# A selective scan with a routed expert layer on one core: another order of VectorE's instructions, and five loads and products placed elsewhere

## The chip, the cores and the metric

One core of one Trainium2 chip runs the whole program. The metric is the device time of one execution in microseconds. In the profile PE is TensorE, DVE is VectorE, ACT is ScalarE, POOL is GpSimd and SP is SyncE, which only issues DMAs.

## What is computed

The input is 2 batch rows of 1024 tokens with 512 values, all in float32. Each token is normalised (layernorm) and goes through two branches; the output is `x + s * g`.

```python
proj = xn @ W_in.T                       # x and gate, 1024 channels each
x = silu(conv4(x))                       # four taps along time, per channel
ts, B, C = rms(x @ W_x.T)                # 32, 16 and 16 values of a token
dt = softplus(ts @ W_dt.T + b_dt)        # per channel and token
state = state * exp(dt * A) + (dt * x) * B      # 16 states of each channel
y = (state . C + x * D) * silu(gate)
s = y @ W_out.T
g = silu(sum of the token's top 2 of 8 experts, weighted by softmax)
```

## The kernel before, in words

**Tiles and quads.** The 2048 tokens are cut into 4 chunks of 512 (two chunks to a batch row), the 1024 channels into 8 groups of 128 that stand on the partitions. A tile n is one chunk c = n // 8 with one group t = n % 8, so the main loop of every engine runs over 32 tiles. A tile has 16 states to each channel. They are done in 4 quads of 4 states; m = 4n + q numbers the quads through the program. For the scan the channels of a group are spread so that 32 channels with 4 states fill the 128 partitions, and a quad is 4 instructions of 128x512 (r = 0 to 3; half 0 is r = 0, 1, the low half; half 1 is r = 2, 3, the high half).

**The life of a quad.** GpSimd makes the drives `(dt*x)*B` for the quad in one instruction (`drives`, L588) into a ring of 4 quads. ScalarE makes the decays `exp(dt*A)` into four banks `sc` of PSUM, two at a time (`decays(m, h)`, L801). VectorE scans each r along time (L1175). Then the scanned states are multiplied by C: the high half by VectorE (`products(m, 1)`, L1185), the low half by GpSimd (`low_products`, L601) where `POOL_QUADS` says so, else by VectorE. TensorE adds them over the states (`sums`, L1426). The four banks `sc` are single: the decays of half h of quad m+1 wait until that half of quad m has been read, which for the high half is the end of its product. In the first chunk of a batch row ScalarE also copies the last column of each scan into `state` (`keep_states`, L780) before it overwrites the half, and GpSimd's low product waits for that copy.

**Step sizes.** For tile n+2 TensorE projects, ScalarE does the exponential and logarithm (`softplus`), and VectorE finishes softplus with three instructions that each need the one before (`step_sizes`, L1154, L1156, L1158) and multiplies by x (`times_x`, L1150). Tiles that are not in `VECTOR_LOG` have the sum done by TensorE, and VectorE only multiplies. ScalarE stores dt and dt*x to DRAM (`keep_rows`, L849), SyncE reads them back spread over the partitions (`spread`, L406), and GpSimd's drives of the tile wait for that.

**The convolution of the next chunk.** In the tiles with t = 2 to 5 (late) and 3 to 6 (early) of the chunks 0 to 2 one group of x of the next chunk is projected by TensorE (`next_x`, L1322, from `w_x`), copied by ScalarE with the first tap (`copy_x`, L707 to L712), and VectorE adds three taps, each on the result of the one before (`convolve`, L1114). ScalarE applies Silu later, with the gate's Silu (`silu_gate`, L861), between two loads of its function table (L941, L949).

**Dependent instructions on VectorE.** Where an instruction of VectorE needs the result of an earlier one, the program waits on a semaphore that the earlier one raises (`link`, or `scan_ok` for a product). In the order before, such an instruction nearly always comes directly behind the one that it waits for: scan, scan, product; tap, tap, tap; the three parts of a step size and the multiplication.

**Each engine's order is written out by hand** in its own loop over the tiles; SyncE's queue is one such list. Of SyncE the change touches the load of `w_out` (2 MB, L474, issued in tile 2, first used in tile 8) and that of `w_x` in tile 18. There the order is: wait for `o_add` (the last sum of an output tile, made by GpSimd), a slot and an expert's weights, more slots, and then `load_w_x`. A slot is 128 gathered tokens of one expert: `x_slot` is loaded by SyncE, turned by TensorE (L1400), copied by ScalarE (L811), multiplied (L1411), copied (L820) and stored (L827). In the tiles 0 and 1 GpSimd scatters token rows into the slots (L552) between the drives.

**A tile's order on VectorE before**, which the change rewrites:

```python
low(m); [times_x(n+1)]; scans(m, 1); [step_sizes(n+1)]; products(m, 1); gate_tile(n-1)
low(m+1); [convolve(early)]; scans(m+1, 1); products(m+1, 1)
low(m+2); high(m+2); [convolve(late)]
low(m+3); high(m+3); [rms or step_sizes(n+2)]
```

## Time and profile before

| | us |
|---|---|
| median of 3 runs (1069.73 to 1072.17) | 1071.06 |
| the profiled execution, its own time | 1074.76 |
| its span, first to last instruction | 1072.9 |
| mean granted clock of TensorE | 0.906 of full speed |

The profiled execution is 3.7 us above the median of the runs and its time is 1.9 us more than its span. The profile gives for each engine the time in which it was busy, so that VectorE and GpSimd, both with high shares, must be read stretch by stretch: idle time of an engine counts only where the chain that ended last passes through what it waited for. The main loop's tiles take 24 to 36 us each.

### The profile page before, as it was taken

To read this page: it belongs to the slowest core of one execution; us is meant where nothing else is said; L and a number is where in the kernel's file an instruction comes from. 1 tells how busy PE (TensorE), PEld (TensorE's weight loads), DVE (VectorE), ACT (ScalarE), POOL (GpSimd) and SP (SyncE) were. 2 spreads that over 40 slices of the span, in tenths; PEclk is the share of its full clock that TensorE was granted. 3 is DMA by queue.
4 is the path that set the end of the run, shared out by engine and by line. 5 is a ranking of instruction groups with operands and counts; after the bars stand their busy time and mean duration, and the time that the engine had idled before them with its cause. 6 is when DMAs were issued, how large, how long until landed. Compare 5 with 4: busy or idle time off the path is not lost.

```text
span 1072.9 us, 10234 instructions
## 1 busy us (share of the span) xinstructions
PE 861.6 (80%) x2756; PEld 319.1 (30%) x2756; DVE 996.6 (93%) x1025; ACT 727.6 (68%) x1281; POOL 909.7 (85%) x322
## 2 busy tenths in 40 slices
PE   8943557988978998898846859889897999679568
PEld 5321112333323333333211313333332343223122
DVE  6779988999999989999999899999999989999997
ACT  3657656788787766788565566688777666567543
POOL 0617898997989998888798979799988988999996
PEclk9976668999999999999876879999998999889779
DMA  9847668767778576666743752965648556664725
GB/s 336 345 158 285 223 235 330 278 247 267 263 266 333 183 270 241 228 257 212 259 113 143 217 194 109 320 231 191 228 149 303 217 215 235 216 220 182 274 42 154
DMA packets 86585, 245.93 MB, mean 229 GB/s; under 512 B 9344, under 2 KB 10752, under 8 KB 79872
## 3 DMA queue, kind: packets, MB, share of 16 engines
q1 hardware_dynamic: 67712, 197.03, 51.4%
q10 hardware_dynamic: 12672, 31.46, 7.4%
q0 software_dynamic: 6144, 16.78, 5.8%
q8 instruction: 23, 0.38, 0.1%
q14 instruction: 34, 0.28, 0.1%
HBM read 183.11 MB, written 62.13 MB: 229 GB/s over the span
## 4 chain that ended last, share of the span: by engine, by line
DVE 30%; PE 22%; POOL 21%; issue 11%; DMA 9%; ACT 5%; SPq 2%; DVEq 0%; ACTq 0%; POOLq 0%
DVE sc_ps L1175 13%; POOL drive L588 12%; DVE drive L1175 8%; PE x_ps L1458 5%; POOL drive L601 4%; PE f_ps L1411 4%; DMA rep<-rep_rows 4%; PE y_ps L1426 3%; PE dt_ps L1386 2%; DMA rep_rows<-dtu 2%; DVE x_ps L1114 2%; DVE drive L1185 2%; PE x_ps L1322 2%; POOL moe L573 2%; ACT sc_ps L801 1%
## 5 line engine op out<-in xcount | busy, mean ns | idle before, releaser
L588 POOL TENSOR_TENSOR drive<-rep,b_all 128x2048 f32<-128x2048 f32 x127 | 578.9, 4598 | 46.6 <-DMA rep<-rep_rows 40.5
L801 ACT ACTIVATE sc_ps<-rep,a_neg 128x512 f32<-128x512 f32 x512 | 332.0, 681 | 93.3 <-DVE drive L1185 63.4
L601 POOL TENSOR_TENSOR drive<-drive,c_all 128x1024 f32<-128x1024 f32 x94 | 224.2, 2385 | 20.6 <-ACT state L780 12.8
L1426 PE MATMUL y_ps<-drive,stack 128*32 128x512 f32 x1024 | 153.5, 675 | 107.1 <-POOL drive L601 59.8
L1175 DVE TENSOR_TENSOR_SCAN sc_ps<-sc_ps,state,drive 128x512 f32<-128x512 f32 x164 | 201.0, 1272 | 4.7 <-ACT sc_ps L801 2.4
L1185 DVE TENSOR_TENSOR drive<-sc_ps,c_all 128x1024 f32<-128x1024 f32 x162 | 198.4, 1224 | 5.4
L1175 DVE TENSOR_TENSOR_SCAN sc_ps<-sc_ps,drive 128x512 f32<-128x512 f32 x160 | 186.5, 1211 | 14.6 <-ACT sc_ps L801 7.4
L1411 PE MATMUL f_ps<-w_ring,xT_slot 128*128 128x512 f32 x368 | 171.8, 611 | 14.9 <-ACT xT_slot L811 14.7
L1386 PE MATMUL dt_ps<-xnT,w_g 128*128 128x512 f32 x232 | 126.8, 697 | 27.5 <-ACT dtu L768 27.5
L1175 DVE TENSOR_TENSOR_SCAN drive<-sc_ps,state,drive 128x512 f32<-128x512 f32 x92 | 112.7, 1266 | 3.4 <-ACT sc_ps L801 3.4
L1175 DVE TENSOR_TENSOR_SCAN drive<-sc_ps,drive 128x512 f32<-128x512 f32 x96 | 111.7, 1205 | 0.0
L1411 PEld LDWEIGHTS f_ps<-w_ring,xT_slot 128*128 128x128 f32 x368 | 68.9, 195 | 117.4 <-issue 116.7
L1322 PE MATMUL x_ps<-xnT,w_x 128*128 128x512 f32 x192 | 90.0, 613 | 3.1 <-DMA w_x<-wx_in 3.1
L1458 PE MATMUL x_ps<-w_out,xy 128*128 128x512 f32 x176 | 83.6, 622 | 0.0
L1386 PEld LDWEIGHTS dt_ps<-xnT,w_g 128*128 128x128 f32 x232 | 49.2, 223 | 110.3 <-issue 110.3
L1426 PEld LDWEIGHTS y_ps<-drive,stack 128*32 128x32 f32 x1024 | 21.5, 113 | 199.5 <-issue 119.1
L780 ACT ACTIVATE state<-sc_ps 128x2 f32<-128x2 f32 x80 | 13.4, 168 | 64.5 <-DVE drive L1185 63.1
L1322 PEld LDWEIGHTS x_ps<-xnT,w_x 128*128 128x128 f32 x192 | 35.6, 193 | 56.9 <-issue 52.1
L1420 PE MATMUL y_ps<-xy,diag 128*128 128x512 f32 x64 | 35.5, 638 | 17.8 <-DVE xy L1202 17.8
L1458 PEld LDWEIGHTS x_ps<-w_out,xy 128*128 128x128 f32 x176 | 32.9, 196 | 51.6 <-issue 51.0
L1363 PE MATMUL dt_ps<-dt_in,w_dt 128*128 128x512 f32 x64 | 42.2, 745 | 5.4 <-DVE dt_in L1225 4.2
L811 ACT COPY xT_slot<-f_ps 128x512 f32<-128x512 f32 x46 | 26.6, 578 | 26.1 <-PE f_ps L1400 26.1
(187 smaller groups left out, 1034.0 us busy)
## 6 DMA issues: line engine op xcount, KB each, us to landing
rep<-rep_rows SPq DMA_DIRECT2D x128, 512.0 KB
w_ring<-wring SPq DMA_DIRECT2D x46, 1024.0 KB, 5.4
rep_rows<-dtu ACTq DMA_DIRECT2D x32, 512.0 KB
x_slot<-slot_x SPq DMA_DIRECT2D x46, 256.0 KB, 7.0
slot_rows<-y_slot ACTq DMA_DIRECT2D x46, 256.0 KB
w_g<-wg_in SPq DMA_DIRECT2D x32, 256.0 KB
w_x<-wx_in SPq DMA_DIRECT2D x24, 256.0 KB
slot_x<-zeros SPq DMA_DIRECT2D x1, 5888.0 KB, 20.5
```

The source lines that it names most:

```text
L588: pool.tensor_tensor(drive[:, m % RING, :, :], rep[:, n % 2, :, 1, :], b_all[:, q:q + 1, :].broadcast_to([P, NR, TC]), ALU.mult).then_inc( ...
L601: pool.tensor_tensor(drive[:, m % RING, 0:2, :], drive[:, m % RING, 0:2, :], c_all[:, q:q + 1, :].broadcast_to([P, 2, TC]), ALU.mult).then ...
L801: act.activation(sc[:, r, :], rep[:, n % 2, r, 0, :], ACT.Exp, scale=a_neg[:, lo:lo + 1]).then_inc(decay_ok, 1)
L1175: dve.tensor_tensor_scan(to, sc[:, r, :], drive[:, m % RING, r, :], state[:, lo:lo + 1] if follows else 0.0, ALU.mult, ALU.add).then_inc(s ...
L1185: dve.tensor_tensor(drive[:, m % RING, 2 * h:2 * h + 2, :], sc[:, 2 * h:2 * h + 2, :], c_all[:, q:q + 1, :].broadcast_to([P, 2, TC]), ALU. ...
L1322: last = pe.matmul(x_bank(j), w(h), xnT[:, c % 2, h, :], start=(h == 0), stop=(h == HK - 1))
L1363: pe.matmul(dt_ps[:, :], w_dt[:, t, :], dt_in[:, :], start=True, stop=True).then_inc(dt_mm, 1)
L1386: mm = pe.matmul(gate_bank(c, t)[:, :], w_g[:, h, :], xnT[:, c % 2, h, :], start=(h == 0), stop=(h == HK - 1))
L1411: last = pe.matmul(f_ps[:, :], xT_slot[:, h, :], w_ring[:, j % 2, h, :], start=(h == 0), stop=(h == HK - 1))
L1420: pe.matmul(y_ps[:, :], diag[:, :], xy[:, c % 2, t, :], start=True, stop=False).then_inc(skip_mm, 1)
L1426: last = pe.matmul(y_ps[CH * r:CH * (r + 1), :], stack[:, :], drive[:, m % RING, r, :], start=False, stop=(m % NQ == NQ - 1))
L1458: last = pe.matmul(bank, xy[:, c % 2, t, P * i:P * (i + 1)], w_out[:, t, :], start=(t == 0), stop=(t == NT - 1))
```

## The change

VectorE's scans are issued one at a time, and other instructions are put between those that depend on each other:
- the three taps stand between the scans of quad m+1 (early) or m+3 (late);
- in the tiles with an early group the first scan of quad m+2 stands ahead of the high product of quad m+1, in those with a late group the first scan of m+3 ahead of the high product of m+2;
- the gate's product of the tile before stands ahead of the high product of quad m, but in the tiles of `GATE_BEHIND` behind it;
- in the 10 tiles of `STEPS_AMONG_SCANS` the three parts of a step size stand among the last scans and products, and the multiplication by x moves behind the first scan of the next tile;
- `times_x` of tiles whose sum TensorE makes stands ahead of the low product.

Besides: ScalarE makes the decays of half 0 of quad m+3 ahead of the late group's `copy_x`; in the 11 tiles of `SILU_SOON` it does the gate's Silu with both table loads ahead of the low decays of quad m+2. In tile 0 both low products that GpSimd made (quads 1 and 2) are VectorE's. SyncE loads `w_out` in tile 4, and `w_x` in tile 18 ahead of the wait for `o_add`.

```diff
--- before.py
+++ after.py
...
 POOL_QUADS = {n: (0, 1, 2) if 7 <= n < 14 else (0, 1, 2, 3) for n in range(TILES) if 2 <= n % (PER_ROW * NT) < 14}
-POOL_QUADS.update({0: (1, 2), 14: (2, 3), 15: (0, 1), 18: (0, 1, 2), 24: (0, 1, 2), 30: (0,)})
+POOL_QUADS.update({14: (2, 3), 15: (0, 1), 18: (0, 1, 2), 24: (0, 1, 2), 30: (0,)})
...
 VECTOR_LOG = (0, 1, 2, 3, 4, 5, 7, 8, 10, 11, 12, 16, 17, 18, 19, 21, 23, 24, 26, 27, 28, 29, 31)
...
+STEPS_AMONG_SCANS = (1, 3, 5, 10, 15, 19, 21, 26, 27, 29)
+GATE_BEHIND = (3, 5, 9, 10, 15, 18, 19, 21, 25, 26, 27, 29, 30)
+SILU_SOON = (7, 8, 9, 23, 24, 25, 26, 27, 28, 29, 30)
...
+        tap_sum, part_ok = sem("tap_sum"), sem("part_ok")
...
-                if n == 2:
+                if n == 4:
                     rows_put(sp, 0)
...
+                        load_w_x(NT * (c + 1) + late_x(c, t) + 1)
                         sp.wait_ge(o_add, TT * c)
...
-                if late_x(c, t) is not None:
+                if late_x(c, t) is not None and (c, t) != (PER_ROW, 2):
                     load_w_x(NT * (c + 1) + late_x(c, t) + 1)
...
                     copy_x(NT * (c + 1) + early)
                 decays(m + 1, 1)
                 copy_slot_T(b, first_slot)
+                if n in SILU_SOON:
+                    act.preload_act_table_set(SILU)
+                    silu_gate(n)
+                    act.preload_act_table_set(LNEXP)
                 decays(m + 2, 0)
-                act.preload_act_table_set(SILU)
-                if left is not None:
-                    silu_x(NT * (c + 1) + left)
-                if early is not None:
-                    silu_x(NT * (c + 1) + early)
-                silu_gate(n)
-                if (c and even and t == 1) or (not even and t == NT - 1):
-                    silu_moe(c - 1, 0, TT)
-                act.preload_act_table_set(LNEXP)
+                if n not in SILU_SOON:
+                    act.preload_act_table_set(SILU)
+                    if left is not None:
+                        silu_x(NT * (c + 1) + left)
+                    if early is not None:
+                        silu_x(NT * (c + 1) + early)
+                    silu_gate(n)
+                    if (c and even and t == 1) or (not even and t == NT - 1):
+                        silu_moe(c - 1, 0, TT)
+                    act.preload_act_table_set(LNEXP)
                 decays(m + 2, 1)
                 copy_slot_y(b, first_slot)
-                if late is not None:
-                    copy_x(NT * (c + 1) + late)
                 store_slot(b, first_slot)
                 if n == 0:
                     scale_rows(0, 2)
                 decays(m + 3, 0)
+                if late is not None:
+                    copy_x(NT * (c + 1) + late)
                 if n == 0:
                     scale_rows(2, 5)
                 copy_slot_T(b, second_slot)
...
+            def tap(j, k):
                 c, t = divmod(j, NT)
-                dve.wait_ge(tap_ok, j + 1)
-                if c == 1:
+                if k == 1:
+                    dve.wait_ge(tap_ok, j + 1)
+                else:
+                    dve.wait_ge(tap_sum, 2 * j + k - 1)
+                if k == K - 1 and c == 1:
                     dve.wait_ge(s_stage, 16 * (NCH - 2))
                     dve.wait_ge(lgT_mm, 1)
-                if c >= 2:
+                if k == K - 1 and c >= 2:
                     dve.wait_ge(o_mm, TT * (c - 1))
+                dve.scalar_tensor_tensor(out=x_bank(j) if k < K - 1 else xy[:, c % 2, t, :], in0=padded(j)[:, k:k + TC],
+                                         scalar=cw[:, t * K + k:t * K + k + 1], in1=x_bank(j),
+                                         op0=ALU.mult, op1=ALU.add).then_inc(tap_sum if k < K - 1 else conv_ok, 1)
+
+            def convolve(j):
                 for k in range(1, K):
-                    tap = dve.scalar_tensor_tensor(out=x_bank(j) if k < K - 1 else xy[:, c % 2, t, :], in0=padded(j)[:, k:k + TC],
-                                                   scalar=cw[:, t * K + k:t * K + k + 1], in1=x_bank(j),
-                                                   op0=ALU.mult, op1=ALU.add)
-                    if k < K - 1:
-                        link(tap)
-                    else:
-                        tap.then_inc(conv_ok, 1)
+                    tap(j, k)
...
+                dve.wait_ge(ln_ok, k + 1)
+                dve.scalar_tensor_tensor(out=dt_ps[:, :], in0=dt_ps[:, :], scalar=0.0, in1=t_e[:, :],
+                                         op0=ALU.max, op1=ALU.add).then_inc(part_ok, 1)
+
+            def less_rounding(k):
+                dve.wait_ge(part_ok, 2 * (k - pe_logs(k)) + 1)
+                dve.scalar_tensor_tensor(out=dt_ps[:, :], in0=t_w[:, :], scalar=-1.0, in1=dt_ps[:, :],
+                                         op0=ALU.add, op1=ALU.subtract).then_inc(part_ok, 1)
+
+            def plus_log(k):
+                dve.wait_ge(part_ok, 2 * (k - pe_logs(k)) + 2)
+                dve.tensor_tensor(dt_ps[:, :], t_l[:, :], dt_ps[:, :], ALU.subtract).then_inc(sp_ok, 1)
+
             def step_sizes(k):
-                dve.wait_ge(ln_ok, k + 1)
-                link(dve.scalar_tensor_tensor(out=dt_ps[:, :], in0=dt_ps[:, :], scalar=0.0, in1=t_e[:, :],
-                                              op0=ALU.max, op1=ALU.add))
-                link(dve.scalar_tensor_tensor(out=dt_ps[:, :], in0=t_w[:, :], scalar=-1.0, in1=dt_ps[:, :],
-                                              op0=ALU.add, op1=ALU.subtract))
-                dve.tensor_tensor(dt_ps[:, :], t_l[:, :], dt_ps[:, :], ALU.subtract).then_inc(sp_ok, 1)
+                larger_part(k)
+                less_rounding(k)
+                plus_log(k)
                 times_x(k)
 
-            def scans(m, h):
+            def scan(m, r):
                 n, q = divmod(m, NQ)
                 c, t = divmod(n, NT)
-                if m == 0 and h == 0:
+                if m == 0 and r == 0:
                     dve.wait_ge(first_half, 1)
-                elif m == 0 or h == 0:
+                elif m == 0 or r == 0:
                     drives_done(dve, m + 1)
                 follows = c % PER_ROW > 0
                 if follows:
-                    dve.wait_ge(state_ok, kept_states(m - NQ * NT) + h + 1)
-                for r in (2 * h, 2 * h + 1):
-                    lo = column(t, q, r)
-                    to = drive[:, m % RING, r, :] if h == 0 and on_pool(m) else sc[:, r, :]
-                    dve.wait_ge(decay_ok, NR * m + r + 1)
-                    dve.tensor_tensor_scan(to, sc[:, r, :], drive[:, m % RING, r, :],
-                                           state[:, lo:lo + 1] if follows else 0.0,
-                                           ALU.mult, ALU.add).then_inc(scan_ok, 1)
+                    dve.wait_ge(state_ok, kept_states(m - NQ * NT) + r // 2 + 1)
+                lo = column(t, q, r)
+                to = drive[:, m % RING, r, :] if r < 2 and on_pool(m) else sc[:, r, :]
+                dve.wait_ge(decay_ok, NR * m + r + 1)
+                dve.tensor_tensor_scan(to, sc[:, r, :], drive[:, m % RING, r, :],
+                                       state[:, lo:lo + 1] if follows else 0.0,
+                                       ALU.mult, ALU.add).then_inc(scan_ok, 1)
...
-            def low(m):
-                scans(m, 0)
+            def low_product(m):
                 if not on_pool(m):
                     products(m, 0)
-
-            def high(m):
-                scans(m, 1)
-                products(m, 1)
...
             route_rows()
-            for h in range(2):
-                scans(0, h)
-                products(0, h)
+            scan(0, 0)
+            scan(0, 1)
+            low_product(0)
+            scan(0, 2)
...
-                    low(m)
+                    scan(m, 0)
+                    if n - 1 in STEPS_AMONG_SCANS:
+                        times_x(n + 1)
+                    scan(m, 1)
                     if pe_log(n + 1):
                         times_x(n + 1)
-                    scans(m, 1)
+                    low_product(m)
+                    scan(m, 2)
+                    scan(m, 3)
                     if chunk_end and not pe_log(n + 1):
                         step_sizes(n + 1)
+                    if n not in GATE_BEHIND:
+                        gate_tile(n - 1)
                     products(m, 1)
-                if n:
-                    gate_tile(n - 1)
-                low(m + 1)
+                    if n in GATE_BEHIND:
+                        gate_tile(n - 1)
+
+                scan(m + 1, 0)
                 if early is not None:
-                    convolve(NT * (c + 1) + early)
-                scans(m + 1, 1)
+                    tap(NT * (c + 1) + early, 1)
+                scan(m + 1, 1)
+                if early is not None:
+                    tap(NT * (c + 1) + early, 2)
+                low_product(m + 1)
+                scan(m + 1, 2)
+                if early is not None:
+                    tap(NT * (c + 1) + early, 3)
+                scan(m + 1, 3)
                 if after_odd and t == 2:
                     out_tile(c - 1, 3)
+                if early is not None:
+                    scan(m + 2, 0)
                 products(m + 1, 1)
-                low(m + 2)
+
+                if early is None:
+                    scan(m + 2, 0)
+                scan(m + 2, 1)
+                low_product(m + 2)
                 if after_odd and t == 1:
                     out_tile(c - 1, 0)
-                high(m + 2)
+                scan(m + 2, 2)
+                scan(m + 2, 3)
                 if late is not None:
-                    convolve(NT * (c + 1) + late)
+                    scan(m + 3, 0)
+                products(m + 2, 1)
                 if after_odd and t == 1:
                     out_tile(c - 1, 1)
-                low(m + 3)
-                high(m + 3)
-                if rms_tile:
+
+                if late is not None:
+                    tap(NT * (c + 1) + late, 1)
+                else:
+                    scan(m + 3, 0)
+                scan(m + 3, 1)
+                if late is not None:
+                    tap(NT * (c + 1) + late, 2)
+                low_product(m + 3)
+                scan(m + 3, 2)
+                if late is not None:
+                    tap(NT * (c + 1) + late, 3)
+                if n in STEPS_AMONG_SCANS:
+                    larger_part(n + 2)
+                scan(m + 3, 3)
+                if n in STEPS_AMONG_SCANS:
+                    less_rounding(n + 2)
+                products(m + 3, 1)
+                if n in STEPS_AMONG_SCANS:
+                    plus_log(n + 2)
+                elif rms_tile:
                     rms(c + 1)
                 elif n + 2 < TILES and not pe_log(n + 2):
                     step_sizes(n + 2)
```

## Rows read from the trace of the kernel before

**Rows 1.** The page, busy time, share of the span and instructions of each engine.
```profile
PE 861.6 (80%) x2756; PEld 319.1 (30%) x2756; DVE 996.6 (93%) x1025; ACT 727.6 (68%) x1281; POOL 909.7 (85%) x322
```
**Rows 2.** The page, the chain that ended last, shares of the span by engine.
```profile
DVE 30%; PE 22%; POOL 21%; issue 11%; DMA 9%; ACT 5%; SPq 2%; DVEq 0%; ACTq 0%; POOLq 0%
```
**Rows 3.** The same chain in order of time: start us, us, what.
```profile
106.33 2.35 POOL drive L601
...
148.20 7.84 DMA rep_rows<-dtu
...
159.21 10.78 DMA x_slot<-slot_x
...
517.58 2.80 DMA slot_rows<-y_slot
...
646.12 2.64 DMA rep_rows<-dtu
...
670.85 5.86 DMA w_x<-wx_in
...
906.58 4.55 POOL drive L588
```
**Rows 4.** Four stretches: us; busy us and count of PE, PEld, DVE, ACT, POOL; clock.
```profile
180.34:299.20 118.86, 106.18 (x350) 38.79 (x348) 117.50 (x119) 96.46 (x188) 110.34 (x33) 1.00 0.72 257
...
420.04:512.13 92.09, 82.79 (x259) 31.43 (x260) 91.15 (x88) 73.22 (x127) 79.62 (x29) 0.98 0.66 233
...
674.69:798.41 123.72, 110.29 (x350) 40.35 (x350) 118.41 (x120) 96.66 (x188) 108.83 (x33) 0.97 0.62 222
...
906.58:1030.45 123.87, 92.78 (x306) 32.65 (x302) 118.13 (x107) 79.48 (x125) 121.46 (x41) 0.86 0.62 213
```
**Rows 5.** VectorE's timeline in tile 13: start us, us, engine, line, what, count.
```profile
490.78 1.52 DVE L1114 SCALAR_TENSOR_TENSOR x_ps<-x_pad,cw,x_ps 128x512 f32<-128x512 f32 x2
492.33 0.75 DVE L1114 SCALAR_TENSOR_TENSOR xy<-x_pad,cw,x_ps 128x512 f32<-128x512 f32 x1
493.00 2.46 DVE L1175 TENSOR_TENSOR_SCAN sc_ps<-sc_ps,state,drive 128x512 f32<-128x512 f32 x2
495.49 1.23 DVE L1185 TENSOR_TENSOR drive<-sc_ps,c_all 128x1024 f32<-128x1024 f32 x1
496.63 2.45 DVE L1175 TENSOR_TENSOR_SCAN drive<-sc_ps,state,drive 128x512 f32<-128x512 f32 x2
```
**Rows 6.** VectorE's timeline at five waits; in brackets idle time before and its releaser.
```profile
137.64 2.35 DVE L1175 TENSOR_TENSOR_SCAN sc_ps<-sc_ps,drive 128x512 f32<-128x512 f32 x2 [4.28 <-POOL drive L588]
...
172.60 2.35 DVE L1175 TENSOR_TENSOR_SCAN sc_ps<-sc_ps,drive 128x512 f32<-128x512 f32 x2 [2.66 <-ACT sc_ps L801]
...
177.53 0.70 DVE L1154 SCALAR_TENSOR_TENSOR dt_ps<-dt_ps,t_e 128x512 f32<-128x512 f32 x1 [1.33 <-ACT t_l L755]
...
407.73 1.55 DVE L1114 SCALAR_TENSOR_TENSOR x_ps<-x_pad,cw,x_ps 128x512 f32<-128x512 f32 x2 [0.90 <-ACT x_ps L710]
...
683.22 0.69 DVE L1202 TENSOR_TENSOR xy<-y_ps,gate 128x512 f32<-128x512 f32 x1 [2.11 <-PE y_ps L1426]
```
**Rows 7.** VectorE's timeline in tile 14, the product ahead of the step size's multiplication.
```profile
514.62 1.23 DVE L1185 TENSOR_TENSOR drive<-sc_ps,c_all 128x1024 f32<-128x1024 f32 x1
515.76 0.68 DVE L1150 TENSOR_TENSOR dtu<-dt_ps,xy 128x512 f32<-128x512 f32 x1
```
**Rows 8.** ScalarE's timeline in tile 7, the gate's Silu and the decays behind.
```profile
313.39 0.60 ACT L861 ACTIVATE gate<-x_ps 128x512 f32<-128x512 f32 x1
314.00 1.28 ACT L949 ACT_TABLE_LOAD   x1
315.30 0.17 ACT L780 ACTIVATE state<-sc_ps 128x2 f32<-128x2 f32 x1
315.50 1.30 ACT L801 ACTIVATE sc_ps<-rep,a_neg 128x512 f32<-128x512 f32 x2
```
**Rows 9.** GpSimd's timeline at the ends of tiles 7 and 23, with idle time before.
```profile
318.06 2.37 POOL L601 TENSOR_TENSOR drive<-drive,c_all 128x1024 f32<-128x1024 f32 x1 [2.20 <-ACT state L780]
...
817.27 2.37 POOL L601 TENSOR_TENSOR drive<-drive,c_all 128x1024 f32<-128x1024 f32 x1 [4.75 <-ACT state L780]
```

4 lines of the change are left out of this document (3 added, 1 removed).

## The prediction

> **What bounds the kernel now.** The page's busy shares come first: VectorE 93%, GpSimd 85%, TensorE 80% [rows 1]. None is full, and the chain that ended last runs through three engines, VectorE 30%, TensorE 22%, GpSimd 21% [rows 2]. So the next view is the busy time by stretch [rows 4]. In tiles 3 to 6 (180.34 to 299.20 us) VectorE works 117.50 of 118.86 us, in tiles 11 to 13 91.15 of 92.09, in tiles 19 to 22 118.41 of 123.72: there VectorE is the bound, and GpSimd has 8.5, 12.5 and 14.9 us free. From 906.58 to 1030.45 it is the other way: GpSimd works 121.46 of 123.87. Between these the chain in order of time goes through DMAs and GpSimd: `rep_rows` at 148.20 and a slot's load at 159.21, a slot's store at 517.58 ahead of the gathers, `w_x` at 670.85, and GpSimd's drives from 906.58 on [rows 3]. A saving on VectorE counts in the first kind of stretch and not in the last.
>
> What VectorE pays for a dependent instruction stands in its timeline [rows 5]. Two scans take 2.46 us from 493.00, to 495.46; the product that needs them starts at 495.49, 0.03 later. The product ends at 496.72, and the next scan, which needs nothing of it, starts at 496.63, 0.09 earlier. The third tap starts at 492.33, 0.03 after the second's end at 492.30, and the scan behind it at 493.00 where the tap ends at 493.08. So an instruction that needs the one ahead costs about 0.03 + 0.09 = 0.12 us more than one that doesn't.
>
> **The change part by part.**
>
> *Parting.* Counted in the two orders of the main loop, instructions that stand directly behind the one that they need fall from 276 to 143. At 0.12 us these 133 are 16.0 us of VectorE's time. What lies on the path: 31 in tiles 3 to 6, 24 in tiles 11 to 13, 31 in tiles 19 to 22 [rows 4], 5 in tile 10 behind 407.73 and 7 in tiles 1 and 2 behind 137.64, together 98, or 98 x 0.12 = 11.8 us. The other 35 stand where GpSimd, TensorE or a DMA sets the pace, or in the start, and count as nothing; their cover is that engine, and without it they are another 4.2 us. In tiles 3 to 6 the cut is 3.7 us and GpSimd has 8.5 us free, in tiles 19 to 22 3.7 of 14.9, so on the mean GpSimd doesn't take over.
>
> *Tile 0.* VectorE makes two more low products, each 1.23 us and 0.03 behind its scan [rows 5], 2.5 us together. They are hidden: ahead of quad 7 VectorE waits 4.28 us for GpSimd's drives [rows 6]. GpSimd loses the product at 106.33, 2.35 us, which stands on the chain [rows 3]; the drives and scatters behind it follow without a gap that something else sets, so quad 7 starts about 2.3 us sooner. VectorE then has 4.3 - 2.5 = 1.8 us of wait left to give, with what parting returns in tile 1 just enough. I take 2.0 us; the bounds are 0 (ScalarE's decays, which now wait for the low products, come too late) and 2.3.
>
> *`w_out` in tile 4.* Behind 148.20 the store of `rep_rows` takes 7.84 us, where the same store takes 2.64 at 646.12, and the slot's load at 159.21 takes 10.78 [rows 3]. SyncE issues the 2 MB of `w_out` just ahead of them. The late slot holds ScalarE and then TensorE, and VectorE waits 2.66 and 1.33 us at 172.60 and 177.53 [rows 6]. The two waits are the upper bound, 4.0 us, since VectorE can't go faster than without waiting. The lower is below nothing: in tile 4 the same bytes stand ahead of the spread of the next dt on SyncE's queue and can make it late by the same 7.84 - 2.64 = 5.2 us; with no gain in tile 2 and that uncovered it is -5.2. GpSimd's 8.5 us free over the four tiles are the cover. I take 3.0, near the upper bound, since that cover is larger than the delay and both waits are of the work that the load delays.
>
> *Tile 10.* The wait of 0.90 us for the late group's first tap at 407.73 [rows 6] is filled by the scan that now stands ahead; 0.9 us, bounds 0 and 0.9.
>
> *Tile 14.* The multiplication by x at 515.76 comes ahead of the low product of 1.23 us at 514.62 [rows 7]. ScalarE's copy of dt and then, in its order, the store of the slot at 517.58 wait for it, and the gathers for that store [rows 3]. 1.15 us, bounds 0 and 1.2.
>
> *`w_x` in tile 18.* The load at 670.85, 5.86 us [rows 3], no longer waits for the output's sum; it waits for the projection that read `w_x` before, which is past by then. The wait of TensorE for it goes, and with it VectorE's 2.11 us at 683.22 [rows 6]. Behind the waits on SyncE's queue stand the same slot loads as before. 2.1 us, bounds 0 and 2.1. What is late next is VectorE itself.
>
> *Silu ahead of the low decays.* In tile 7 the Silu with its two table loads of 1.28 us stands ahead of the state copy at 315.30 and the high decays [rows 8]; GpSimd's low product waits 2.20 us at 318.06 for a later copy, and 4.75 us at 817.27 in tile 23 [rows 9]. The block of 1.28 + 0.60 + 1.28 = 3.2 us moves into time in which ScalarE waited. The drives behind these products also need the next tile's dt from DRAM, which no row here dates: 0 to 2.2 us in each tile, and I take 0.7 in each, 1.4. In tiles 8, 9 and 24 to 30 TensorE or GpSimd is the bound and I take nothing; uncovered, VectorE would wait the 3.2 us for its low decays wherever the gate's projection is late.
>
> *New waits.* The high product of quad m+1 stands one scan later in 12 early tiles, that of m+2 in 12 late ones. After the early one VectorE has one scan, 1.24 - 0.09 = 1.15 us, until it needs the high decays. ScalarE needs for the first of these 0.20 us for the state copy and half of a pair of 1.30 [rows 8], with the start about 1.0. The margin of 0.15 us is thin. I take a loss of 0.1 us for 12 tiles, rounded to 1.0; the bounds are 0 and, where ScalarE isn't free, the whole 1.15 each time.
>
> The sum: 11.8 + 2.0 + 3.0 + 0.9 + 1.15 + 2.1 + 1.4 - 1.0 = 21.4 us. The profiled execution took 1074.8 us, so its like would take 1053.4; against the median of 1071.06, which lies 3.7 us lower, 1049.7.
>
> **A rule that speaks against it.** The rows show 0.12 us between a dependent and an independent pair [rows 5]. The Trainium skill (VectorE: DVE Perf Modes, The DRAIN you can't avoid) says that the next instruction doesn't start until the pipe has emptied, that a semaphore after each costs nothing extra, and that only the number of instructions counts. By it parting would be worth nothing. Here the trace disagrees: the scan at 496.63 starts 0.09 us before the product ends.
>
> **The rivals.**
>
> 1. *GpSimd takes over.* Where all four low products of a tile are GpSimd's, a shorter tile may wait for the spread dt or for its products. For it: the multiplication by x comes one scan later in ten places, and the dt goes through two DMAs before the drives. Against it: 8.5 and 14.9 us free [rows 4]. Then the 7.4 us of tiles 3 to 6 and 19 to 22 are not gained: 1049.7 + 7.4 = 1057.1. Chance 0.16.
> 2. *The load of `w_out` only moves its delay*: the 3.0 us go, perhaps with 5.2 more; 1052.7 to 1057.9. For it: in tile 4 SyncE's queue is as full. Against it: the cover of 8.5 us. Chance 0.10.
> 3. *Parting is worth nothing*, by the rule above as a mechanism: an instruction that follows another kind starts at its end, dependent or not. Then the 11.8 us go, 1061.5. Against it speak the pairs of one and of two kinds in [rows 5], which cost alike. Chance 0.06.
> 4. *Slower: the decays come back late.* The high product stands one scan later in 24 places, and the decays, TensorE's sums and, through the ring, the drives wait for it. If each place costs its scan of 1.2 us, that is 28.8 us, and 1049.7 + 28.8 = 1078.5. It decides against the change from 0.9 us a place (21.4 / 24). For it: the margin of 0.15 us. Against it: where this margin lies ScalarE waits rather than VectorE, and behind the late ones two scans and taps follow. Chance 0.07.
> 5. *Nothing happens*: the orders are the same for the chip. The diff moves instructions in fact, so this needs gains and losses to cancel. Chance 0.02.
>
> The forecast has the rest, 0.59.
>
> **How the numbers follow.** The likeliest case gives 1049.7. Its best end takes the upper bounds and no new wait: 21.4 + 0.3 + 1.0 + 0.05 + 3.0 + 1.0 = 26.8, or 1044.3, and 2 us less where half of the 35 covered pairs count: 1042. Above, the range takes in rivals 1 and 2 and reaches to rival 3, 1062. What lies outside is rival 4, rival 5 and a part of rival 3. Of this kernel a difference of 0.2% (2.1 us) can be told from no change. Faster by more than that: 0.59 + 0.16 + 0.10 + 0.06 = 0.91; within it 0.02; slower 0.07.
>
> **What would show it right or wrong.** In the profile after: VectorE busy about 16 us less plus 2.5; the stretches of tiles 3 to 6 and 19 to 22 shorter by 3.7 us each and still full; no wait of VectorE between 137 and 180 us beyond 1 us; `rep_rows` near 148 us landing in about 3 us; no wait of TensorE for `w_x`; the last stretch, GpSimd's, as long as before. It is wrong if taps and scans start no earlier than before relative to their neighbours, if VectorE's waits for `sc_ps` of ScalarE grow by some us in the tiles with an early group, or if GpSimd's waits for `rep` in tile 4 or 5 reach VectorE.

## The result, and the profile of the changed kernel

The changed kernel took 1054.95 us (median of 4 runs, 1053.23 to 1056.37), the kernel before beside it 1071.62: 16.7 us less, ratio 0.9844 with a 95% interval of 0.9820 to 0.9868. In a second comparison, without any edit, it took 1057.12 against 1069.70, ratio 0.9885 (0.9870 to 0.9901), or 12.6 us less. The forecast was 1049.7 in a range of 1042 to 1062. So the kernel is faster, by the forecast's main cause, but by 13 to 17 us where the sum of the terms said 21.4. The profiled execution took 1055.66 us for a span of 1053.8, 0.7 above its median, where that of before lay 3.7 above; between the two profiles lie 19.1 us.

The page of the changed kernel, the busy times and then the chain that ended last by engine, to be held against [rows 1] and [rows 2]:

```profile
PE 851.3 (81%) x2756; PEld 316.7 (30%) x2756; DVE 986.1 (94%) x1027; ACT 727.2 (69%) x1281; POOL 905.0 (86%) x320
...
POOL 27%; PE 24%; DVE 18%; issue 11%; DMA 10%; ACT 7%; SPq 2%; ACTq 0%; DVEq 0%; POOLq 0%
```

VectorE is busy 10.5 us less than in [rows 1]; with the two low products of tile 0 added (2.5) the parting took some 13 us off it, where the forecast wanted to see 16. The count of the pairs was right: in the main loop 284 of VectorE's instructions start 0.03 to 0.04 us after the end of the one ahead in before, and 150 in the changed kernel. But of the 0.12 us of a pair only 0.09 are time in which VectorE is busy (two instructions that now overlap); the other 0.03 were a gap. VectorE was the largest engine of the chain at 30%; now it has 18%, and GpSimd leads. The same four stretches as [rows 4], taken between the same scans (tiles 3 to 6, 11 to 13, 19 to 22, and the last one as near as it can be matched):

```profile
173.39:293.38 119.99, 107.79 (x350) 39.68 (x350) 115.24 (x120) 96.27 (x187) 112.16 (x35) 0.99 0.75 272
411.81:501.10 89.29, 80.19 (x264) 30.10 (x257) 89.19 (x89) 73.78 (x129) 81.47 (x28) 1.00 0.66 237
662.27:779.81 117.54, 107.66 (x351) 39.45 (x349) 115.56 (x121) 96.46 (x188) 109.29 (x33) 0.99 0.66 234
887.01:1010.60 123.59, 89.66 (x305) 31.72 (x306) 119.12 (x109) 79.93 (x126) 121.39 (x41) 0.88 0.64 216
```

Tiles 11 to 13 are 2.8 us shorter and VectorE works 89.19 of 89.29 us: 24 parted pairs at 0.12 are 2.9. The match is partly luck: the multiplication by x of a step size (0.67 us) has moved from tile 10 into tile 11, so the same work became about 3.4 us shorter, 0.14 a pair; the taps themselves are 0.01 to 0.03 us shorter too. Tiles 19 to 22 are 6.2 shorter. The last stretch, GpSimd's, is as long as before. Tiles 3 to 6, where 3.7 us were forecast, are 1.1 us **longer**: VectorE's busy time fell by 2.3 us, but it now idles 4.75 us where it idled 1.36. (In a second profile of the same kernel they are 1.0 us shorter than before; experiment 8 says why.) The rest of the gain lies mostly ahead of tile 3 (7.0 us), in tile 10 (33.97 to 31.01) and in tile 15 (33.47 to 32.11).

That the parting does what it says is seen in VectorE's timeline in tile 13 (the answer to [rows 5]; start us, us, engine, line, what):

```profile
478.36 1.27 DVE L1197 TENSOR_TENSOR_SCAN drive<-sc_ps,state,drive 128x512 f32<-128x512 f32 x1
479.55 0.73 DVE L1126 SCALAR_TENSOR_TENSOR x_ps<-x_pad,cw,x_ps 128x512 f32<-128x512 f32 x1
480.19 1.28 DVE L1197 TENSOR_TENSOR_SCAN drive<-sc_ps,state,drive 128x512 f32<-128x512 f32 x1
481.39 0.73 DVE L1126 SCALAR_TENSOR_TENSOR x_ps<-x_pad,cw,x_ps 128x512 f32<-128x512 f32 x1
...
485.05 1.26 DVE L1197 TENSOR_TENSOR_SCAN drive<-sc_ps,state,drive 128x512 f32<-128x512 f32 x1
486.23 1.20 DVE L1207 TENSOR_TENSOR drive<-sc_ps,c_all 128x1024 f32<-128x1024 f32 x1
```

The scan at 478.36 would end at 479.63, and the tap starts at 479.55; the product at 486.23 starts 0.08 ahead of the end of the scan before it. The taps and the product started 0.03 behind before.

VectorE's timeline at its waits up to tile 7 (in brackets idle time and releaser; the answer to [rows 6]):

```profile
134.84 2.35 DVE L1197 TENSOR_TENSOR_SCAN sc_ps<-sc_ps,drive 128x512 f32<-128x512 f32 x2 [0.54 <-POOL drive L593]
...
161.74 1.23 DVE L1197 TENSOR_TENSOR_SCAN drive<-sc_ps,drive 128x512 f32<-128x512 f32 x1 [0.18 <-ACT sc_ps L806]
...
180.52 0.69 DVE L1219 TENSOR_TENSOR xy<-y_ps,gate 128x512 f32<-128x512 f32 x1 [1.31 <-PE y_ps L1487]
...
191.77 2.35 DVE L1197 TENSOR_TENSOR_SCAN sc_ps<-sc_ps,drive 128x512 f32<-128x512 f32 x2 [0.75 <-ACT sc_ps L806]
194.29 1.22 DVE L1197 TENSOR_TENSOR_SCAN drive<-sc_ps,drive 128x512 f32<-128x512 f32 x1 [0.18 <-ACT sc_ps L806]
...
250.82 2.35 DVE L1197 TENSOR_TENSOR_SCAN sc_ps<-sc_ps,drive 128x512 f32<-128x512 f32 x2 [0.74 <-ACT sc_ps L806]
...
287.09 2.35 DVE L1197 TENSOR_TENSOR_SCAN sc_ps<-sc_ps,drive 128x512 f32<-128x512 f32 x2 [0.83 <-ACT sc_ps L806]
...
308.74 2.34 DVE L1197 TENSOR_TENSOR_SCAN drive<-sc_ps,drive 128x512 f32<-128x512 f32 x2 [0.56 <-ACT sc_ps L806]
```

The 4.28 us for the drives are 0.54, and the two waits of tile 2 are gone. New are waits for ScalarE of 0.7 to 0.8 us in tiles 3, 5 and 6, of 0.56 in tile 7, and rows of 0.18 at the first scan of quad 3. What `w_out` does in its new place stands in the chain in order of time (start us, us) and in GpSimd's timeline of the same stretch:

```profile
207.24 7.35 DMA rep_rows<-dtu
216.45 7.71 DMA rep<-rep_rows
```

```profile
215.27 2.35 POOL L606 TENSOR_TENSOR drive<-drive,c_all 128x1024 f32<-128x1024 f32 x1
224.33 4.53 POOL L593 TENSOR_TENSOR drive<-rep,b_all 128x2048 f32<-128x2048 f32 x1 [6.71 <-PE y_ps L1487]
```

The store of `rep_rows` for tile 5 takes 7.35 us (2.64 at 646.12 in [rows 3]), and GpSimd stands still 6.71 us. The bracket names TensorE; the last of the four spreads landed at 224.16 (216.45 + 7.71), and that is what ended the wait.

In tile 2, which the load has left, the store was to land in about 3 us by the forecast. It did not. ScalarE issues it, and SyncE's spread waits for it (ScalarE's, then SyncE's timeline in after):

```profile
146.82 0.33 ACTq L854 DMA_DIRECT2D rep_rows<-dtu  x1
```

```profile
153.37 3.33 SPq L410 DMA_DIRECT2D rep<-rep_rows  x4
```

That is 6.5 us, where it was 7.84 with `w_out` beside it: at this place only 1.3 us of the store's delay belong to `w_out`, and what causes the rest is not shown. What went is the late slot (TensorE's timeline in before, then in after):

```profile
170.03 1.11 PE L1400 MATMUL f_ps<-ident,x_slot 128*128 128x128 f32 x4 [6.25 <-DMA x_slot<-slot_x]
```

```profile
163.44 0.66 PE L1461 MATMUL f_ps<-ident,x_slot 128*128 128x128 f32 x4 [1.70 <-DMA x_slot<-slot_x]
```

### The profile page after: what moved, and what is told of

Read it like the earlier page. It is cut to its first block, busy times and chain, and to the rows that moved or that the text cites. A ratio compares the mean times of both kernels' runs of the same rounds, so it can differ in the third digit from the quotient of the medians.

```text
span 1053.8 us, 10364 instructions
## 1 busy us (share of the span) xinstructions
PE 851.3 (81%) x2756; PEld 316.7 (30%) x2756; DVE 986.1 (94%) x1027; ACT 727.2 (69%) x1281; POOL 905.0 (86%) x320
## 4 chain that ended last, share of the span: by engine, by line
POOL 27%; PE 24%; DVE 18%; issue 11%; DMA 10%; ACT 7%; SPq 2%; ACTq 0%; DVEq 0%; POOLq 0%
POOL drive L593 16%; DVE sc_ps L1197 7%; POOL drive L606 6%; PE x_ps L1519 5%; DMA rep<-rep_rows 5%; PE f_ps L1472 4%; DMA rep_rows<-dtu 3%; DVE drive L1197 3%; PE dt_ps L1447 3%; DVE drive L1207 3%; PE y_ps L1487 3%; ACT sc_ps L806 2%; PE x_ps L1383 2%; POOL slot_x L557 2%; POOL moe L578 2%
## 5 line engine op out<-in xcount | busy, mean ns | idle before, releaser
L606 POOL TENSOR_TENSOR drive<-drive,c_all 128x1024 f32<-128x1024 f32 x92 | 219.7, 2388 | 10.1 <-ACT state L785 10.0
L1197 DVE TENSOR_TENSOR_SCAN sc_ps<-sc_ps,drive 128x512 f32<-128x512 f32 x164 | 193.4, 1214 | 9.2 <-ACT sc_ps L806 5.2
L1447 PE MATMUL dt_ps<-xnT,w_g 128*128 128x512 f32 x232 | 120.5, 667 | 23.5 <-ACT dtu L773 23.5
L1487 PEld LDWEIGHTS y_ps<-drive,stack 128*32 128x32 f32 x1024 | 21.4, 112 | 201.1 <-issue 138.4
L1424 PE MATMUL dt_ps<-dt_in,w_dt 128*128 128x512 f32 x64 | 39.9, 709 | 5.4 <-DVE dt_in L1242 4.2
L628 POOL TENSOR_SCALAR rep<-rep,moe 128x512 f32<-128x512 f32 x8 | 16.5, 2066 | 30.5 <-DVEq L1144 30.5
L773 ACT COPY dtu<-dt_ps 128x512 f32<-128x512 f32 x32 | 18.7, 584 | 33.3 <-DVE dtu L1162 33.3
```

The lines of the kernel that those rows point to most:

```text
L606: pool.tensor_tensor(drive[:, m % RING, 0:2, :], drive[:, m % RING, 0:2, :], c_all[:, q:q + 1, :].broadcast_to([P, 2, TC]), ALU.mult).then ...
L1197: dve.tensor_tensor_scan(to, sc[:, r, :], drive[:, m % RING, r, :], state[:, lo:lo + 1] if follows else 0.0, ALU.mult, ALU.add).then_inc(s ...
L1424: pe.matmul(dt_ps[:, :], w_dt[:, t, :], dt_in[:, :], start=True, stop=True).then_inc(dt_mm, 1)
L1447: mm = pe.matmul(gate_bank(c, t)[:, :], w_g[:, h, :], xnT[:, c % 2, h, :], start=(h == 0), stop=(h == HK - 1))
L1487: last = pe.matmul(y_ps[CH * r:CH * (r + 1), :], stack[:, :], drive[:, m % RING, r, :], start=False, stop=(m % NQ == NQ - 1))
```

## The experiments

The questions: how much is the parting worth by itself, and is the rest additive; did the load of `w_out` only move its delay (rival 2); what eats the parting in tiles 3 to 6; and are the small terms the size that the forecast gave them. "After" is the changed kernel.

**1. Everything but the parting.** VectorE's order as before, all else as in after.

```diff
--- after
+++ this run
...
-                    scan(m, 0)
-                    if n - 1 in STEPS_AMONG_SCANS:
-                        times_x(n + 1)
-                    scan(m, 1)
+                    low(m)
...
-                scan(m + 1, 0)
+                low(m + 1)
                 if early is not None:
-                    tap(NT * (c + 1) + early, 1)
...
+                    convolve(NT * (c + 1) + early)
+                scans(m + 1, 1)
...
+                low(m + 3)
+                high(m + 3)
```

> The changed kernel with VectorE's order of the main loop as it was before; all other parts of the change stay. Theory A (an instruction directly behind the one that it needs costs 0.12 us more, and this is on the path in the stretches that VectorE bounds): VectorE busy about 16 us more than in the changed kernel, tiles 11 to 13 together 2.8 us longer, the whole 8 to 11 us slower than the changed kernel, so 1063 to 1066. Rival B (the gain comes from the moved loads and products, parting is worth nothing): 1054 to 1057, tiles 11 to 13 unchanged.

1065.37 us, ratio 0.9941 (0.9919 to 0.9962), 6.4 us under before. Tiles 11 to 13 are 2.8 us longer than in after, as theory A said; VectorE is busy 12.2 us more, not 16.

**2. The parting alone.** VectorE's new order; GpSimd's products, `w_out`, `w_x` and Silu as before.

```diff
-POOL_QUADS.update({14: ...
+POOL_QUADS.update({0: (1, 2), 14: ...
...
-SILU_SOON = (7, 8, 9, 23, 24, 25, 26, 27, 28, 29, 30)
+SILU_SOON = ()
...
-                if n == 4:
+                if n == 2:
...
-                        load_w_x(NT * (c + 1) + late_x(c, t) + 1)
                         sp.wait_ge(o_add, TT * c)
...
-                if late_x(c, t) is not None and (c, t) != (PER_ROW, 2):
+                if late_x(c, t) is not None:
```

> VectorE's new order alone (with ScalarE's copy of the late group behind the decays, which belongs to it); w_out in tile 2, w_x behind the wait, the Silu behind the low decays and GpSimd's two products in tile 0 as before. Theory A: faster than before by the parted places on the path, 8 to 11 us, so 1061 to 1064; tiles 3 to 6 shorter by up to 3.7 us if nothing but VectorE bounds them. Rival B: within 2 us of before, 1070 to 1073.

1061.9 us, ratio 0.9903 (0.9879 to 0.9927), 9.9 us under before. Tiles 3 to 6 (busy time by stretch), first of the kernel with the old order, then of the one with the parting alone:

```profile
176.30:295.20 118.90, 107.46 (x349) 39.16 (x347) 117.54 (x119) 96.68 (x187) 110.31 (x33) 0.99 0.75 270
```

```profile
179.35:295.98 116.63, 105.47 (x349) 38.50 (x347) 114.84 (x119) 96.33 (x188) 111.71 (x34) 1.00 0.73 262
```

The old order takes 118.9 us there, as before, whether `w_out` loads in tile 2 or 4. The new one takes 116.6 with the load in tile 2, and with it in tile 4 120.0 in the first profile of after and 117.9 in the second. So the parting works there too (2.2 of 3.7 us with the load in tile 2); the moved load takes 1.3 us of it back in tile 5, and the other 2.1 us of the first profile arise with TensorE's clock in tile 3 (experiment 8). The two halves add: 9.9 + 6.4 = 16.3 against 16.7. The 9.9 us are of the whole order, with the wait that it fills in tile 10 and the multiplication that it brings forward in tile 14, and not of the parted pairs alone; those are seen by themselves in tiles 11 to 13.

Rival 3, the parting worth nothing, is refuted. The Trainium skill (VectorE: DVE Perf Modes, Rules for kernel authors) advises to minimize the number of VectorE's instructions and not their semaphores; here the number is the same, and the order is worth 9.9 us. The forecast gave the page's rule more sharply than it stands. The section that it names in the Trainium skill (VectorE: DVE Perf Modes, The DRAIN you can't avoid) itself adds that a next instruction that is not held starts earlier. The trace agrees: independent instructions start 0.08 to 0.09 us before the end of the one ahead. That a semaphore costs nothing extra was measured there with one kind of copy, and the trace disagrees for the pairs here, which cost 0.12 us more where one waits for the other.

**3. `w_out` back in tile 2, and in tile 6.**

```diff
-                if n == 4:
+                if n == 2:
```

The second kernel has `n == 6` in this line.

> The changed kernel with w_out loaded in tile 2 again. Theory C (in tile 4 the load only moves its delay: the spread dt of tile 5 lands about 6 us late, GpSimd's low products lag, and TensorE and ScalarE behind them hold VectorE in tiles 5 and 6): GpSimd idle in tile 4 falls from 6.9 to below 2 us, tiles 4 to 6 are 2 to 4 us shorter, and about as much is lost again in tile 2; in all 1054 to 1057. Rival D (the missing 4.8 us of tiles 3 to 6 are the thin margin of the scan ahead of the high product): tiles 3 to 6 stay as long as in the changed kernel, 122 us without what tile 2 leaves behind, and the whole is 3 us slower, 1058.

> The changed kernel with w_out loaded in tile 6, two tiles ahead of its first use. Theory C: GpSimd idle in tile 4 below 2 us, tiles 4 and 5 together 1.5 to 3 us shorter; unless the same delay comes up in tile 6 the whole gains 1 to 3 us, 1052 to 1054. Rival D: tiles 3 to 6 as in the changed kernel, 1055.

In tile 2: 1055.54 us, ratio 0.9858 (0.9837 to 0.9880). In tile 6: 1057.21, ratio 0.9861 (0.9840 to 0.9881), where 1052 to 1054 were expected. Neither can be told from after's 0.9844. With the load in tile 2 VectorE waits in its timeline as before:

```profile
169.56 1.23 DVE L1197 TENSOR_TENSOR_SCAN sc_ps<-sc_ps,drive 128x512 f32<-128x512 f32 x1 [2.49 <-ACT sc_ps L806]
...
174.49 0.70 DVE L1166 SCALAR_TENSOR_TENSOR dt_ps<-dt_ps,t_e 128x512 f32<-128x512 f32 x1 [0.67 <-ACT t_l L760]
```

Tile 2 is 32.47 us long instead of 29.03. But tile 3 takes 29.10 instead of 31.40 (of which 2.3 are not the load's, see experiment 8) and tile 5 30.07 instead of 31.14, GpSimd idles 1.6 us in tile 4 instead of 6.9, and tile 9 starts at 351.14 us in both kernels. The move is worth nothing by then: rival 2, in its milder form. Tile 5 takes 30.1 us in all four kernels with VectorE's new order that don't load the whole `w_out` in tile 4, and 30.6 to 32.5 in the eight that do. With the load in tile 6 tile 7 starts 2.6 us sooner than in after, and tile 8 takes 31.24 us instead of 29.62, so that 0.9 us is left at tile 9.

**4. GpSimd's two products in tile 0 kept.**

```diff
-POOL_QUADS.update({14: ...
+POOL_QUADS.update({0: (1, 2), 14: ...
```

> The changed kernel with the low products of quads 1 and 2 on GpSimd again. By the prediction's step: quad 7 starts about 2.0 us later than in the changed kernel (134.84 there), and the whole is 2 us slower. Rival: GpSimd, which stands without a gap from quad 7 to quad 18, carries the 2.3 us on, so that GpSimd's drives of tile 3 and TensorE's sums behind come later too and tiles 2 to 4 lose more than 2.3 us.

1058.42 us, ratio 0.9874 (0.9840 to 0.9908). The wait of quad 7 is back in VectorE's timeline:

```profile
137.65 2.35 DVE L1197 TENSOR_TENSOR_SCAN sc_ps<-sc_ps,drive 128x512 f32<-128x512 f32 x2 [4.36 <-POOL drive L593]
```

137.65 against 134.84 is 2.8 us, above the forecast's upper bound of 2.3 at this place. Tile 4 starts 1.5 us later than in after, tile 9 0.6, and the span is 1.0 us longer; the runs give 3 us with intervals that overlap. The 2.0 of the forecast are true where it looked, and by tile 9 most of them are spent.

**5. The load of `w_x` behind the output's sum again.**

```diff
-                        load_w_x(NT * (c + 1) + late_x(c, t) + 1)
                         sp.wait_ge(o_add, TT * c)
...
-                if late_x(c, t) is not None and (c, t) != (PER_ROW, 2):
+                if late_x(c, t) is not None:
```

> The changed kernel with w_x in tile 18 behind the wait for the output's sum again. By the prediction's step TensorE waits 2 to 4 us for it and tile 19 is 2.1 us longer than its 29.70; since VectorE comes through tile 19 faster now, it may be more, up to 3.9 us as tile 19 shows in the kernel with the new order alone (33.57). Rival: the load lands in time now that VectorE's tiles are shorter; tile 19 unchanged.

1060.01 us, ratio 0.9889 (0.9852 to 0.9925). TensorE's timeline, then VectorE's:

```profile
665.96 5.40 PE L1382 MATMUL x_ps<-xnT,w_x 128*128 128x512 f32 x8 [3.06 <-DMA w_x<-wx_in]
```

```profile
672.42 0.69 DVE L1218 TENSOR_TENSOR xy<-y_ps,gate 128x512 f32<-128x512 f32 x1 [3.15 <-PE y_ps L1486]
```

TensorE waits 3.06 us for the load, and its eight matmuls behind that wait take 5.40 us at a mean granted clock of 0.68 of full speed; in after the same eight follow without a wait and take 3.60 us. (In before it was as here, 3.06 and 5.40 us.) Tile 19 takes 33.84 us instead of 29.70. The span is 4.0 us longer, so the move is worth 4.1 us, where the forecast had 2.1 from VectorE's wait of before. Both are right: with VectorE's old order tile 19 gains 2.3 us (34.07 to 31.73) from the move. The parting alone gains 0.5 us there (33.57), since it only lengthens the wait; together they gain 4.4.

**6. The gate's Silu nowhere ahead.**

```diff
-SILU_SOON = (7, 8, 9, 23, 24, 25, 26, 27, 28, 29, 30)
+SILU_SOON = ()
```

> The changed kernel with the gate's Silu behind the low decays in all tiles. By the prediction's step: GpSimd's last low product but one of tiles 7 and 23 starts up to 1.5 us later and the drives of the next chunk with it, 0 to 1.5 us each, 1.4 together; tiles 24 to 30 the same length, since TensorE and GpSimd bound them. Rival: no effect at tiles 7 and 23, and in tiles 26 to 29 VectorE's and GpSimd's waits shift: GpSimd is the bound there and the sum of these tiles (109 us from 898.8 minus 2) changes by more than 1 us.

1056.98 us, ratio 0.9850 (0.9824 to 0.9876), not to be told from after. Tile by tile: tile 7 takes 27.57 us instead of 28.13 and tile 23 26.36 instead of 26.93, so the early Silu **costs** 0.57 in each: the wait at 308.74 above. Tile 26 takes 28.60 instead of 29.63 (but 29.79 in the kernel of experiment 2, which has no Silu ahead either, so this one is not sure). What it gives back lies in tile 30, 31.98 instead of 30.45, where VectorE waits longer for GpSimd's drive (VectorE's timeline of this kernel, then of after, at the same scan):

```profile
1012.87 2.47 DVE L1197 TENSOR_TENSOR_SCAN sc_ps<-sc_ps,state,drive 128x512 f32<-128x512 f32 x2 [2.92 <-POOL drive L593]
```

```profile
1010.60 2.47 DVE L1197 TENSOR_TENSOR_SCAN sc_ps<-sc_ps,state,drive 128x512 f32<-128x512 f32 x2 [1.39 <-POOL drive L593]
```

The span is 1.8 us longer, but 1.2 of it arise in tiles 19 to 21, where the Silu stands alike in both kernels. What belongs to the Silu is about 0.6 us net: 1.6 lost in tiles 23 and 26 against 2.2 won in tiles 27 to 30, while tile 7's loss is gone by tile 9. The place of the gain holds over the kernels: tiles 27 to 30 take 111.2 to 112.8 us in the nine kernels with all of `SILU_SOON`, and 113.3 to 114.0 in the three without. Its size is not to be told from noise in the runs.

**7. No scan ahead of the high product in the tiles with an early group.**

```diff
-                if early is not None:
-                    scan(m + 2, 0)
                 products(m + 1, 1)
-                if early is None:
-                    scan(m + 2, 0)
+                scan(m + 2, 0)
```

> The changed kernel without the scan of quad m+2 ahead of the high product of quad m+1 in the 12 tiles with an early group. Theory E (the thin margin costs more than the parting gives in tiles 3, 5, 20 and 21, where VectorE waits 0.75 and 0.18 us for the decays): those waits go, tiles 3 to 6 and 19 to 22 are 1 to 3 us shorter together, tiles 11 to 13 0.12 us longer each; the whole 0 to 2 us faster. Rival F (the waits come from ScalarE's block with the table loads, which ends late because TensorE is late): the waits stay at 0.6 to 0.8 us, each of the 12 tiles is 0.12 us longer, and the whole 1 to 1.5 us slower.

1055.44 us, ratio 0.9849 (0.9811 to 0.9886), span 1053.0: no measurable effect, and neither theory comes out whole. Tiles 11 and 12 are 0.15 us longer each. The wait ahead of quad 2's high scans, which is where the thin margin lies, stays: 0.60 us in tile 5 (0.74 in after) and 0.60 in tile 20 (0.16). So the scan ahead is not what makes ScalarE late there. The rows of 0.18 in tiles 2, 5, 20 and 21 stay too; they stand at the first scan of quad 3, the one that the late group puts ahead of a product, which this edit leaves alone. Tile 3 was 29.10 us here against 31.40, but it was so with the scan ahead as well, in the kernel with the late `w_x` (29.10, an edit far behind tile 3) and when the changed kernel ran again (below).

**8. The changed kernel again.**

> The changed kernel without any edit, to see which of its stretches repeat. If VectorE's 2.27 us of idle time in tile 3 belong to the change (the theory that the late keep_rows is the price of the new order), tile 3 is again 31.4 us long. If they are the luck of a DMA in tiles 1 to 3 (tile 3 was 29.1 us in three kernels with the same order of VectorE and 31.4 in another), it may be 29.1 to 29.5, with tile 4's start between 203 and 206.5. Tiles 6 (29.54), 7 (28.14), 11 to 13 (29.77, 29.76, 29.76), 19 (29.70) and 23 (26.93) repeat within 0.1 us by both. Time 1055 +- 1.5 us, ratio about 0.985.

1057.12 us, ratio 0.9885 (0.9870 to 0.9901), span 1053.6. Tile 3 took 29.10 us with VectorE idle 0.18, where the first profile had 31.40 and 2.27, while tiles 1 and 2 took 1.6 us more between them; tile 4 starts within 0.6 us in both. So the 2.3 us are not a fixed price of the new order. TensorE's timeline, in the first profile and in this one, shows where they arise:

```profile
174.33 5.13 PE L1383 MATMUL x_ps<-xnT,w_x 128*128 128x512 f32 x8 [2.42 <-DMA w_x<-wx_in]
```

```profile
174.68 3.70 PE L1383 MATMUL x_ps<-xnT,w_x 128*128 128x512 f32 x8 [1.95 <-DMA w_x<-wx_in]
```

The load lands no later in the first. But there TensorE had waited 2.42 us, and the eight matmuls behind take 5.13 us at a mean granted clock of 0.72 (0.50, the lower level of 1.2 GHz, from 174.4 to 176.5 us); here it had waited 1.95 us, and they take 3.70 at 1.00. VectorE's wait of 1.31 us at 180.52 is for the sums behind these matmuls. The other two kernels with a tile 3 of 31.3 to 31.4 us, those of experiment 6 and of the two halves in experiment 10, have the same pair, waits of 2.31 and 2.38 us and then 5.40 us of matmuls; in the nine with 29.1 to 29.4 us TensorE had waited 2.02 us at most, and the matmuls take 3.70. Why the wait is sometimes the longer one is not shown. Tiles 5 to 13 repeat within 0.2 us each: the waits of tiles 5, 6 and 7 belong to the kernel.

**9. The second slot's copy behind the last decays in tiles 6 and 22.** Ahead of VectorE's wait at 287.09 ScalarE itself stands, for TensorE's turn of a slot (ScalarE's timeline in after):

```profile
285.21 0.59 ACT L816 COPY xT_slot<-f_ps 128x512 f32<-128x512 f32 x1 [1.80 <-PE f_ps L1461]
...
286.37 1.30 ACT L806 ACTIVATE sc_ps<-rep,a_neg 128x512 f32<-128x512 f32 x2
```

In before ScalarE stood as long at the same copy, but VectorE was still at its earlier scans and product and came to the next ones without a wait (ScalarE's timeline in before, then VectorE's):

```profile
290.96 0.58 ACT L811 COPY xT_slot<-f_ps 128x512 f32<-128x512 f32 x1 [1.87 <-PE f_ps L1400]
```

```profile
289.56 1.23 DVE L1185 TENSOR_TENSOR drive<-sc_ps,c_all 128x1024 f32<-128x1024 f32 x1
290.70 2.33 DVE L1175 TENSOR_TENSOR_SCAN drive<-sc_ps,drive 128x512 f32<-128x512 f32 x2
```

```diff
-                copy_slot_T(b, second_slot)
+                if n not in (6, 22):
+                    copy_slot_T(b, second_slot)
                 if rms_tile:
                     rms(c + 1)
                 decays(m + 3, 1)
+                if n in (6, 22):
+                    copy_slot_T(b, second_slot)
```

> The changed kernel, but in tiles 6 and 22 ScalarE copies the second slot's turned x (L816) behind the last quad's high decays instead of ahead of them. Theory (what ate part of the parting in tiles 3 to 6 and 19 to 22 is ScalarE's queue: in the trace of after ScalarE stands 1.80 us at 285.21 for TensorE's turn, its decays come out behind that copy, and VectorE, which no longer loses time on dependent instructions, waits 0.83 us at 287.09 for them): VectorE's wait of 0.83 us goes in tiles 6 and 22, each of the two tiles is 0.6 to 0.8 us shorter (28.8 where after has 29.54), tiles 7 and 23 start that much earlier, and the time is about 1 us under after's 1054.95. Rival (TensorE is what is late: the expert behind the turn now waits for the later copy, and holds the sums and through the ring the drives): the wait of 0.8 us comes back in tiles 7 and 23 or one quad later, tiles 6 and 7 together as long as in after (57.68 us), time as after or 1 to 2 us longer.

1055.94 us, ratio 0.9867 (0.9851 to 0.9883), against 0.9885 of after beside it. ScalarE's timeline, then VectorE's:

```profile
285.12 0.15 ACT L785 ACTIVATE state<-sc_ps 128x2 f32<-128x2 f32 x1
285.31 1.30 ACT L806 ACTIVATE sc_ps<-rep,a_neg 128x512 f32<-128x512 f32 x2
286.55 0.58 ACT L816 COPY xT_slot<-f_ps 128x512 f32<-128x512 f32 x1
```

```profile
286.18 2.32 DVE L1200 TENSOR_TENSOR_SCAN sc_ps<-sc_ps,drive 128x512 f32<-128x512 f32 x2
```

The scan comes without a wait, and tiles 6 and 22 take 28.60 us instead of 29.54, as the theory said. So ScalarE's order is what holds VectorE there; tile 7 is as long as in after (28.14 us), and the rival is out. The total gains nothing that can be measured: tile 8 takes 30.31 us instead of 29.62, tile 27 28.12 instead of 27.34, and tile 5, which lies ahead of the edit, 32.46 instead of 31.14. The place is shown, the gain isn't.

**10. Three edits together, then with `w_out` in two halves.** Edits 7 and 9, and the Silu back in its old place in tiles 7, 9, 23 and 26; in tile 30 it stays ahead. The second kernel loads one half of `w_out` in tile 4 and one in tile 6, behind that tile's spread. Of the lines shown the last two are in both kernels, the others in the second alone; edits 7 and 9 are left out.

```diff
-                if n == 4:
-                    rows_put(sp, 0)
-                    for half in range(2):
-                        sp.dma_start(w_out[:, ...half...], wring[E + half])
...
                     clear_slots(1, *CLEARS[n])
+                if n in (4, 6):
+                    rows_put(sp, 0)
+                    half = n // 2 - 2
+                    sp.dma_start(w_out[:, ...half...], wring[E + half])
...
-SILU_SOON = (7, 8, 9, 23, 24, 25, 26, 27, 28, 29, 30)
+SILU_SOON = (8, 24, 25, 27, 28, 29, 30)
```

> The changed kernel with three edits together: the high product of quad m+1 again ahead of the scan in tiles with an early group (0.8 us by the span when tried alone), the gate's Silu back behind quad 2's low decays in tiles 7, 9, 23, 26 and 30 kept as changed save these (0.57 us of tile 7, 0.57 us of tile 23 and 1.0 us of tile 26 in the kernel without any early Silu), and the second slot's copy behind the last decays in tiles 6 and 22 (about 1 us). If they add: span 1050.5 to 1051.5 against 1053.8, time about 1052. If each is only moved into the next wait of tiles 8 to 10, where TensorE sets the pace, and 24 to 26: 1054 to 1055, not to be told from the changed kernel.

> The kernel before it (three edits together) and the load of w_out cut in two: one half in tile 4 and one in tile 6, each behind the tile's spread and its w_g, where the changed kernel issues both ahead of tile 4's spread. Theory (the 2 MB delay the store of rep_rows beside them by 4 to 5 us wherever they stand, and this reaches VectorE only where GpSimd has no slack): rep(5) is spread by about 220 us instead of 224.17, GpSimd's idle time in tile 4 falls from 6.9 us to under 3, tile 9 starts 0 to 1 us earlier, time 0 to 1 us less than without the cut. Rival (the second half comes late for the output's first matmul in tile 8, as with the whole load in tile 6, where tile 8 was 1.6 us longer): tile 8 31.2 us instead of 29.6, no gain.

Three edits: 1056.15 us, ratio 0.9870 (0.9854 to 0.9886), span 1053.4, not to be told from after. In tiles 5 to 7 they gain 1.9 us over the first profile of after, and tile 8 takes back 1.6 of it, 31.22 us instead of 29.62. Its rows, GpSimd's and TensorE's timelines, and then TensorE's in after:

```profile
314.93 13.57 POOL L593 TENSOR_TENSOR drive<-rep,b_all 128x2048 f32<-128x2048 f32 x3 [1.27 <-DMA rep<-rep_rows]
```

```profile
323.78 5.37 PE L1447 MATMUL dt_ps<-xnT,w_g 128*128 128x512 f32 x8 [2.04 <-ACT dtu L773]
```

```profile
325.31 3.67 PE L1447 MATMUL dt_ps<-xnT,w_g 128*128 128x512 f32 x8 [2.04 <-ACT dtu L773]
```

GpSimd's first drive of the second chunk starts at 314.93 in place of 314.85, though VectorE starts tile 8 1.5 us sooner: GpSimd now waits 1.27 us for the spread dt, which comes through two DMAs. And the eight matmuls of the gate take 5.37 us instead of 3.67, in a tile whose mean granted clock is 0.95 instead of 1.00. In tile 8 GpSimd, idle 0.5 us in both kernels, sets the pace. The slower matmuls don't: with the cut below they take 3.67 us again, and tile 8 is still 30.76 us long.

With the cut: 1053.94 us, ratio 0.9850 (0.9836 to 0.9864), 3.2 us under after on the same chip, and the intervals don't touch. GpSimd's drive for tile 5 waits for the DMA 1.65 us instead of 6.71, tile 5 takes 30.07 us, and tile 8 30.76, so the rival is half true as well: tile 9 starts at 351.10, where it started. At the start of tile 14 the two kernels of this experiment stand at 501.60 and 501.51, so the cut is worth nothing by then, and the 1.3 us between their spans arise behind tile 14, where it doesn't act. The gain of 3.2 us over after is thus not traced to an edit; and since after gave 0.9844 in the first comparison, whether this version beats the changed kernel is not settled.

## Why the forecast was right, and where it was not

**What bounds the kernel, and the price of a dependent pair** were right: 0.12 us a pair gave 2.9 us for tiles 11 to 13, which came as 2.8, or about 3.4 for the same work. The sign "VectorE busy about 16 us less" was misread: of the 0.12 us only 0.09 are busy time, 133 x 0.09 = 12.0, and 12.2 and 12.6 were measured in experiments 1 and 2.

**The halves.** The terms of VectorE's order (11.8 + 0.9 + 1.15 - 1.0 = 12.85) came as 9.9 us, those of the rest (2.0 + 3.0 + 2.1 + 1.4 = 8.5) as 6.4. Each half is about a quarter short.

**Parting, tiles 3 to 6** failed: 3.7 us forecast, 1.1 lost in one profile and 1.0 gained in the other. The step "GpSimd has 8.5 us free, so on the mean it doesn't take over" looked at the wrong cover. Rival 1's 7.4 us were not lost by GpSimd's pace: with `w_out` in tile 2 2.2 of 3.7 came, and 0.9 more in tile 6 in another kernel, with ScalarE's copy moved. One place where time goes is ScalarE's queue: a copy that waits 1.8 us for TensorE stands ahead of decays that VectorE, one scan sooner, now needs. In before ScalarE waited as long, and VectorE did not wait behind it (experiment 9). The others are the load of `w_out`, in tile 5, and TensorE's clock, in tile 3 of the first profile; the forecast has no term for the clock.

**Tile 0**: 2.0 forecast, 2.8 at quad 7, about 1 us in the span.

**`w_out` in tile 4** failed: 3.0 forecast, no difference measured. The step at fault is the cover: 8.5 us free over four tiles were set against a delay in one. In before 6.4 of these 8.5 us lay in tile 5 and only 1.0 in tile 4. After the change GpSimd idles 6.9 us in tile 4 for the spread dt, catches up in tile 5 with no idle time at all, and VectorE pays 0.74 us at 250.82, tile 5 1.1 us. The forecast's own bound, the store of `rep_rows` late by 5.2 us, was met nearly to the letter in tile 4: 7.35 - 2.64 = 4.7, and in the four kernels with the new order that issue no part of `w_out` ahead of it that store takes 2.7 to 3.1. In tile 2 the same 5.2 us were wrongly put down to `w_out`: the store still takes 6.5 us without it.

**Tile 10 and tile 14**: tile 10 shrank by 2.7 us with the parting alone, where 0.9 and five pairs, 1.5 together, were forecast. Of the other 1.2 0.6 are the multiplication that moved into tile 11, and 0.4 are three more parted pairs, which the forecast had not counted as on the path. Tile 14 shrank by 0.86 in six of the twelve kernels with the new order, where 1.15 were forecast, but by 0.03 in the first profile of after, where VectorE waits 0.73 us for ScalarE at 527.36.

**`w_x` in tile 18**: 2.1 forecast and 2.3 measured with VectorE's old order, 4.1 with the new one. The bound "0 to 2.1" left out that the parting lengthens the very wait that this move takes away (2.11 us at 683.22 in before, 3.15 without the move in experiment 5).

**Silu ahead** failed in its place: 0.7 gained in each of tiles 7 and 23 forecast, 0.57 lost in each. Its gain lies in tiles 27 to 30, to which the forecast gave nothing, and about 0.6 us are left net.

**New waits**: 1.0 us in 12 early places forecast, from a thin margin ahead of quad 2's high scans. In after there is no wait at eight of the 12 places; it is 0.75 us in tile 3 of the first profile only, 0.74 in tile 5, and 0.16 and 0.22 in tiles 20 and 21, and for tiles 5 and 20 experiment 7 shows that the scan ahead is not the cause. The late places, which were counted as free, have waits of 0.14 to 0.18 us each in tiles 2 to 5 and 19 to 21. Not foreseen were 0.83 in tiles 6 and 22 each, and 0.56 in tiles 7 and 23.

**The yardstick** may have cost some more. The forecast took the 3.7 us by which the profiled execution of before lay above its median off the changed kernel too; that one's profile lay only 0.7 above its median. In the profile of before tile 22 has 1.83 us of VectorE's idle time, and with the old order in experiment 1 it has 0.31. By the profiles the error is 21.4 against 19.1, by the medians 21.4 against 16.7 and 12.6. There is one profile of before, so how much of this is chance stays open.

**The sum** came nearer than its terms. `w_x` and tile 10 gave 3.2 us more than forecast (0.6 of it lent by tile 11), and that hides as much of what `w_out` and tiles 3 to 6 failed to give; this part is luck.

Of the signs named beforehand, two did not come: tiles 3 to 6 are not shorter by 3.7 us, and the store near 148 us does not land in about 3 us. And one of the signs of being wrong did: GpSimd's wait for the spread in tile 4 reached VectorE in tile 5. Rival 4, late decays throughout, did not come. Rival 2 came in its milder form, and rival 1's loss came in part, in tiles 3 to 6, by other causes.

## What to carry to other kernels

Where an engine is full, put an independent instruction between each pair that depends; it was worth 0.12 to 0.14 us a pair where VectorE set the pace. Then look at the queues of the engines that serve it: every instruction in them that waits for a third engine should stand behind the work that the fast one now needs sooner. A gain ahead of a stretch that another engine or a DMA paces is lent, not given; read what is left of it at the next such point (here the start of tile 9), not where it arises. And profile the changed kernel twice before explaining a stretch: 2.3 us of tile 3 were in one profile and not in the other.

## What the runs showed that was not expected

- The store of 512 KB in tile 4 takes 2.7 to 3.1 us without `w_out` ahead of it and 7.1 to 7.6 with it in the new order, and the spread behind it starts as much later. But the store in tile 2 takes 6.5 us without `w_out` beside it, so that not every slow store is a large load's doing. Half of the load, issued behind tile 4's spread, left the store at 2.7 us.
- The same eight matmuls of the gate took 3.67 us or 5.37 us in the same tile of two kernels, behind the same wait of 2.04 us, in stretches with a mean granted clock of 1.00 and 0.95. So a tile that starts sooner can still take 1.7 us longer at TensorE. In tile 3 the same two values go with the length of TensorE's wait: 3.70 us of matmuls after waits of up to 2.02 us, 5.13 to 5.40 after 2.31 to 2.42.
- The same kernel was 16.7 and 12.6 us faster than before in two comparisons, with intervals of 0.982 to 0.987 and 0.987 to 0.990, though the spans of its two profiled executions agree within 0.2 us. The interval of one comparison does not hold all of the spread.
